# A gather moved into the attention, the last split halved over two engines, and a wait for output moved into the next block

## What is computed

```python
xn = _layernorm(x)
qkv = xn @ Wqkv + bqkv                       # 16 heads of 16
scores = where(abs(i - j) <= 64, q @ k.T / 4, lowest)
attn = softmax(scores) @ v
attention = attn @ Wout + bout
logits = xn @ router_w + router_b            # 8 experts
gating = softmax(logits, all but the top 2 masked out)
h_e = relu(xn @ w1[e] + b1[e])               # 256 -> 1024, for each expert e
moe = sum over e of gating[:, e] * (h_e @ w2[e] + b2[e])
out = x + attention + moe
```

## Time and profile before

| | us |
|---|---|
| median of 3 runs | 963.66 (963.28 to 963.79) |
| the profiled execution, its time | 962.66 |
| its span, first to last instruction | 960.5 |
| PE busy in the span | 901.5 (94%) |
| VectorE busy | 821.9 (86%) |
| ScalarE busy | 739.9 (77%) |
| POOL busy | 494.6 (51%) |
| mean granted TensorE clock | 0.984 |

### The profile page before, as it was taken

How to read it: one execution, slowest core, us unless ns; L and a number is a source line. 1 busy time by engine, 2 the same in 40 slices (tenths; PEclk the granted TensorE clock), 3 DMA queues, 4 the chain that set the end, 5 groups by cost and what they waited for, 6 DMA issues and landing times. The chain is left out here.

```text
span 960.5 us, 27552 instructions
## 1 busy us (share of the span) xinstructions
PE 901.5 (94%) x7684; PEld 874.9 (91%) x7684; DVE 821.9 (86%) x2171; ACT 739.9 (77%) x1983; POOL 494.6 (51%) x699
## 2 busy tenths in 40 slices
PE   4899799899999999999947999999999999999996
PEld 4788789889999999999947999999999999999996
DVE  5876699998888888888846999999999999999995
ACT  4445799889999999999935777777777777677773
POOL 5220013236565555555443666666666666666663
PEclk9999799999999999999987999999999999999999
DMA  4879433344444445444314222222212223222220
GB/s 147 324 276 311 146 78 94 108 124 136 135 134 141 142 136 150 138 133 135 101 46 165 38 39 43 40 41 41 33 29 43 47 46 48 43 44 35 34 24 1
DMA packets 69867, 95.33 MB, mean 99 GB/s; under 512 B 15549, under 2 KB 48960, under 8 KB 69696
## 3 DMA queue, kind: packets, MB, share of 16 engines
q1 hardware_dynamic: 52800, 77.97, 26.4%
q0 software_dynamic: 17024, 16.88, 11.1%
HBM read 62.91 MB, written 35.53 MB: 102 GB/s over the span
## 5 line engine op out<-in xcount | busy, mean ns | idle before, releaser
L1007 ACT ACTIVATE weights_qkv<-weights_qkv,low 128x256 f32<-128x256 f32 (+1 forms) x512 | 240.3, 480 | 1.4 <-DVE low L818 1.4
L1419 ACT ACTIVATE hid<-ps_experts,b_s 128x256 f32<-128x256 f32 x312 | 130.9, 473 | 115.4 <-PE ps_experts L1486 92.2
L1305 POOL DMA_INDIRECT out<-y,target x78 | 149.2, 1912 | 110.5 <-DVE y L1385 94.2
L829 DVE TENSOR_TENSOR pt<-ps_attend,pt 128x512 fp32r<-128x512 f32 (+1 forms) x256 | 158.5, 620 | 39.2 <-ACT pt L1020 26.1
L1097 PE MATMUL ps_attend<-pt,v_m 128*80 128x256 f32 (+7 forms) x1536 | 187.0, 271 | 2.3 <-DVE inv_t L842 1.0
L1502 PE MATMUL ps_experts<-w_hi,h_hi 128*128 128x256 f32 x624 | 175.5, 281 | 1.1 <-DVE h_lo L1352 1.1
L1486 PE MATMUL ps_experts<-xgt_hi,w_hi 128*128 128x256 f32 x624 | 173.3, 278 | 1.7 <-DVE xgt_lo L1343 1.7
L1097 PEld LDWEIGHTS ps_attend<-pt,v_m 128*80 128x80 f32 (+3 forms) x1536 | 170.7, 161 | 4.2 <-issue 4.2
L1486 PE MATMUL ps_experts<-xgt_hi,w_lo 128*128 128x256 f32 x624 | 173.2, 278 | 0.0
L1486 PE MATMUL ps_experts<-xgt_lo,w_hi 128*128 128x256 f32 x624 | 173.0, 277 | 0.0
L1502 PE MATMUL ps_experts<-w_lo,h_hi 128*128 128x256 f32 x624 | 172.4, 276 | 0.0
(11 more groups left out here) (165 smaller groups left out, 2007.9 us busy)
## 6 DMA issues: line engine op xcount, KB each, us to landing
weights_qkv<-in_w SPq DMA_DIRECT2D x15, 1024.0 KB, 6.7
qk_hi<-weights_qkv SPq DMA_DIRECT2D x16, 512.0 KB, 4.7
qk_lo<-weights_qkv SPq DMA_DIRECT2D x16, 512.0 KB, 5.7
q_st<-qk_hi SPq DMA_DIRECT2D x128, 64.0 KB
k_st<-qk_hi SPq DMA_DIRECT2D x128, 64.0 KB
weights_qkv<-in_x SPq DMA_DIRECT2D x8, 512.0 KB, 4.7
xn_rows<-weights_qkv SPq DMA_DIRECT2D x8, 512.0 KB, 5.3
k_st<-qk_lo SPq DMA_DIRECT2D x64, 64.0 KB
```

The source lines that it names most:

```text
L829: v.tensor_tensor(lo[:, f:l], ps[:, bank_t[h], 0:l - f], hi[:, f:l].bitcast(F32), ALU.subtract).then_inc(s_plo, 1)
L1007: ins = act.activation(wt[:, ring, at_tile(i)], wt[:, ring, at_tile(i)], ACT.Exp, bias=low[:, ring, i:i + 1], scale=-1.0, accum_out=total[ ...
L1305: pool.indirect_dma_start(out_tokens, bass.IndirectOffsetOnAxis(ap=target[:, h:h + 1], axis=0), y[:, h], None, bounds_check=T - 1, oob_is_ ...
L1419: ins = act.activation(hid[:, n % 2, j], ps[:, bank_h[n], j * ROWS:(j + 1) * ROWS], ACT.Relu, bias=b1[:, ds(e * FC + 2 * n + j, 1)])
```

## The change

1. The last chunk of the attention: VectorE normalises it in two halves of 256 tokens, ACT makes `a_hi` half by half, VectorE makes `a_lo` half by half, and PE's last products wait for the half that they read. POOL has no part in it any more.
2. The rows of step 0 are gathered by POOL at the end of its queue in the attention, into a buffer `first_rows` that outlives the block and is set to zero in norm_project. `xg(0)` is that buffer in the experts; rings 1 and 2 are a smaller tile, which POOL sets to zero itself at the start of the experts.
3. SP doesn't wait in the attention for the last stores. Their semaphores outlive the block, and SP waits for them before it loads b2, POOL before its first step.
4. `hid`, `gated_b2` and `y` are allocated ahead of `b2`.

```diff
@@ norm_project, POOL
                 pool.memset(g.late, 0.0)
+                pool.memset(g.first_rows[:].bitcast(F32), 0.0)
@@ attend, SP
                 start(sp, by["sp"])
+                start(sp, s_out)
...
                 sp.wait_ge(s_rows, 16 + START)
-                for h in range(2):
-                    sp.wait_ge(s_out[h], 16 * B + START)
                 sp.wait_ge(s_wload, 32 * (E - 1) + 16 + START)
@@ attend, POOL
-                split_output(B - 1, 1, False)
+                pool.wait_ge(s_rows, 16 + START)
+                pool.tensor_copy(g.first_index[:], g.rows[:, 0:2, 0].bitcast(U32)).then_inc(s_first, 1)
+                pool.wait_ge(s_first, 1 + START)
+                for h in range(2):
+                    pool.indirect_dma_start(
+                        g.first_rows[:, h].bitcast(F32), None, g.xn_dram,
+                        bass.IndirectOffsetOnAxis(ap=g.first_index[:, h:h + 1], axis=0),
+                        bounds_check=T - 1, oob_is_err=False).then_inc(g.s_g[h], 16)
@@ attend, VectorE
-                normalise(2 * B - 1)
+                v.wait_ge(s_pv, HC * 2 * B + START)
+                v.wait_ge(s_invs, 2 * B + START)
+                for h in range(2):
+                    v.tensor_tensor(inv_t[:, half_of(h)], ps[:, bank_o, half_of(h)], inv_t[:, half_of(h)], ALU.mult
+                                    ).then_inc(s_enda, 1)
+                for h in range(2):
+                    v.wait_ge(s_endhi, h + 1 + START)
+                    v.tensor_tensor(a_lo[:, 1, half_of(h)], inv_t[:, half_of(h)],
+                                    a_hi[:, 1, half_of(h)].bitcast(F32), ALU.subtract).then_inc(s_endlo, 1)
@@ attend, ACT
                 inverse_out(2 * B - 1, False)
+                act.wait_ge(s_proj, 2 * (B - 1) + START)
+                for h in range(2):
+                    act.wait_ge(s_enda, h + 1 + START)
+                    act.activation(a_hi[:, 1, half_of(h)], inv_t[:, half_of(h)], ACT.Copy).then_inc(s_endhi, 1)
@@ attend, PE, project
-                        if k % 6 == 0 or k == here[0]:
+                        if bank != bank_m and k == 6:
+                            pe.wait_ge(s_endlo, h + 1 + START)
+                        elif k % 6 == 0 or k == here[0]:
@@ experts, tiles
+        hid = sb("hid", [P, 2, 2, ROWS])
+        gated_b2 = sb("gated_b2", [P, 2, D])
+        y = sb("y", [P, 2, D])
         b2 = sb("b2_s", [P, E, D])
...
-        xg = sb("xg", [P, RING, 2, D], F32R)
+        more_rows = sb("more_rows", [P, RING - 1, 2, D], F32R)
@@ experts, SP
                 sp.wait_ge(s_tr, 1 + START)
+                for h in range(2):
+                    sp.wait_ge(g.s_out[h], 16 * B + START)
                 sp.dma_start(b2[:], g.b2.partition_broadcast(P)).then_inc(s_b2, 16)
@@ experts, POOL
-                pool.wait_ge(s_xz, RING + START)
-                for n in range(RING):
+                for ring in range(1, RING):
+                    pool.memset(xg(ring)[:].bitcast(F32), 0.0).then_inc(s_xz, 1)
+                pool.wait_ge(s_xz, RING - 1 + START)
+                for h in range(2):
+                    pool.wait_ge(s_g[h], 16)
+                for n in range(1, RING):
                     gather(n, n, n)
                     for h in range(2):
                         pool.wait_ge(s_g[h], 16 * n + 16)
+                for h in range(2):
+                    pool.wait_ge(g.s_out[h], 16 * B + START)
@@ experts, VectorE
-                for ring in range(RING):
-                    v.memset(xg[:, ring].bitcast(F32), 0.0).then_inc(s_xz, 1)
```

More of the change, by code:

```diff
@@ L561, in attend @@
         s_xb = [sem("s_xb0", "sp"), sem("s_xb1", "sp")]
-        s_out = [sem("s_out0", "sp"), sem("s_out1", "sp")]
+        s_out = g.s_out
         s_wload = sem("s_wload", "sp")
@@ L593, in attend @@
         s_rows = sem("s_rows", "sp")
+        s_first = sem("s_first", "pool")
+        s_enda = sem("s_enda", "v")
+        s_endhi = sem("s_endhi", "act")
+        s_endlo = sem("s_endlo", "v")
         s_sent = ctx.enter_context(nc.semaphore("s_sent"))
@@ L601, in attend, with half_of @@
         out_rows = g.out.rearrange("b (t p) d -> b p t d", p=P)
+        def half_of(h):
+            return slice(2 * P * h, 2 * P * (h + 1))
         def at_tile(i):
@@ L1213, in experts @@
         xt_lo = sb("xgt_lo", [P, DC, ROWS], F32R)
-        hid = sb("hid", [P, 2, 2, ROWS])
         h_hi = sb("h_hi", [P, FC, ROWS], F32R)
         h_lo = sb("h_lo", [P, FC, ROWS], F32R)
-        gated_b2 = sb("gated_b2", [P, 2, D])
-        y = sb("y", [P, 2, D])
         s_b1 = sem("s_b1", "sp")
@@ L1225, in experts @@
         s_landed = sem("s_landed", "sp")
-        s_xz = sem("s_xz", "v")
+        s_xz = sem("s_xz", "pool")
         s_ident_r = sem("s_ident_r", "v")
         s_idx = sem("s_idx", "pool")
-        s_g = [dma_sem("s_g0"), dma_sem("s_g1")]
+        s_g = g.s_g
         s_tr = sem("s_tr4", "pe")
@@ L1250, in experts, with xg @@
         out_tokens = g.out.rearrange("b n d -> (b n) d")
+        def xg(ring):
+            return more_rows[:, ring - 1] if ring else g.first_rows
         def final(s, ahead=1):
@@ L1283, in gather @@
                     pool.tensor_copy(index[:, ring], g.rows[:, ds(2 * row_step, 2), 0].bitcast(U32)).then_inc(s_idx, 1)
-                    pool.wait_ge(s_idx, s + 1 + START)
+                    pool.wait_ge(s_idx, s + START)
                     pool.sem_inc(g.tick, 1)
@@ L1287, in gather @@
                         pool.indirect_dma_start(
-                            xg[:, ring, h].bitcast(F32), None, g.xn_dram,
+                            xg(ring)[:, h].bitcast(F32), None, g.xn_dram,
                             bass.IndirectOffsetOnAxis(ap=index[:, ring, h:h + 1], axis=0),
                             bounds_check=T - 1, oob_is_err=False).then_inc(s_g[h], 16)
-                pool.wait_ge(s_xz, RING + START)
-                for n in range(RING):
+                for ring in range(1, RING):
[4 more added lines that the diff above has]
+                for n in range(1, RING):
                     gather(n, n, n)
@@ L1471, in transpose_rows @@
                             ins = pe.transpose(ps[:, bank_t, (c * 2 + h) * P:(c * 2 + h + 1) * P].bitcast(F32R),
-                                               xg[:, ring, h, c * P:(c + 1) * P], ident_r[:])
+                                               xg(ring)[:, h, c * P:(c + 1) * P], ident_r[:])
                     ins.then_inc(s_tr, 1)
@@ L1553, in build @@
         g.rows = sb("rows", [P, HT, 2])
+        g.first_rows = sb("first_rows", [P, 2, D], F32R)
+        g.first_index = sb("first_index", [P, 2], U32)
+        g.s_g = [ctx.enter_context(nc.semaphore(f"s_g{h}")) for h in range(2)]
+        g.s_out = [ctx.enter_context(nc.semaphore(f"s_out{h}")) for h in range(2)]
         g.step_expert = sb("step_expert", [P, STEPS], I32)
```

## The result

The changed kernel takes 956.93 us (median of 4 runs, 955.02 to 957.31), the kernel before, on the same chip, 963.47 (4 runs, 962.12 to 963.79). The ratio is 0.9935, 95% interval [0.9921, 0.9948]. I forecast 953.3 and a range of 950.9 to 956.2, so the direction is right and the size is not: 6.5 us of gain where I summed 10.4. The profiled execution took 957.17 us with a span of 955.1, against 962.66 and 960.5: 5.4 us of span.

A forecast was written before the change was run, and what follows sets the result against it. It took the experts' steps as bound by TensorE and sought the gain in the 27.3 us around the change of stage: 1.6 + 2.1 + 7.1 - 0.4 = 10.4 us, so 953.3 us, range 950.9 to 956.2.

The forecast's parts named there:

- Part 1: Attention's tail: normalising and splitting in halves without POOL brings TensorE's next product sooner; gain 1.6 us, ends 0.5 to 2.0.
- rival B: Attention's tail: VectorE's two-input subtraction waits out a POOL gather issue on the shared port; 1.1 lost, 954.4; chance 0.12.
- Part 2: Attention's end: SP no longer waits for the last output to land, so the experts start sooner; gain 2.1 us.
- Rival C: Block's end waits for stores or new gather in flight without being told; 2.1 comes back, 955.4; chance 0.10.
- Part 3: Experts' start: first gather hidden in the attention; entry (R) to first expert matmul falls from 11.57 to 4.5, gain 7.1.
- rival E: Experts: step 1's gather comes late beside b2 and weight loads; at 4 us late 955.4; chance 0.05.
- rival F: Experts' steps: VectorE becomes the bound because tiles lie at other addresses; slower, 968.9; chance 0.02.
- The clock: Experts' start: TensorE's clock still falls, low 4.5 us instead of 3.7; loss 0.4, ends gain 1.85 to loss 3.2.
- my signs of being wrong: Transposes waiting for a gather, first stage over 8 us, subtraction over 0.3 us late, or waiting for step 1's gather.

The follow-up runs named there:

- run 7: The split in halves alone, added to the kernel before: 961.35 us, ratio 0.9990.
- run 5: The changed kernel with SyncE's landing wait for the last stores put back in the attention: 955.82 us, ratio 0.9932.
- run 4: The changed kernel with the last batch's two stores issued some 20 us early, sending a weight tile instead: 954.68 us, ratio 0.9920.
- before again: The kernel before, unchanged, profiled once more: 963.17 us (12 runs), ratio 1.0005.
- run 8: The changed kernel with the split in halves undone, so that GpSimd splits first and gathers then: 959.82 us, ratio 0.9973.
- run 10: The changed kernel with GpSimd waiting for its own gather to land before it leaves the attention: 955.71 us, ratio 0.9933.
- run 12: The changed kernel with the table's 66 small scatters left out; experts' rows are skipped: 954.18 us (one run).
- run 13: The kernel before with the table's 66 small scatters left out; experts' rows are skipped: 960.93 us (one run).
- run 11: The kernel of run 7 with GpSimd waiting for its own last addition before it leaves the attention: 962.26 us (one run).
- run 3: The changed kernel with step 0's gather issued earlier, between the heads of the attention's last batch: 954.03 us, ratio 0.9910.
- run 6: The changed kernel with both the gather issued early and SyncE's landing wait put back: 956.71 us, ratio 0.9932.
- run 9: The changed kernel with one small gather more, issued and awaited at the end of the normalisation and projections block: 954.92 us (one run).
- the square of runs: The changed kernel with gather late or early, without or with landing wait; R-n 7.26 (neither), 7.32 (wait), 4.99 (early gather), 7.31 (both).

## Why the prediction missed

**Part 1, the halves: right.** 1.7 at TensorE where I wrote 1.6, in the changed kernel and alone (run 7). VectorE had been idle for 0.21 when its subtraction began at 492.16; by the trace's records that is 0.03 after the end of ScalarE's first pass (492.13), while GpSimd's second issue (491.79 to 492.80) was running, so that rival B did not occur. The Trainium skill's rule of the shared port pair ("SBUF — State Buffer", "SBUF: two separate sides") would allow a loss of up to one issue here; this trace shows no hold of VectorE.

**Part 2, the landing wait: the step that failed.** I wrote "SP no longer waits 2.1 us; it leaves the block with the second store issued", and from that a gain of 2.1 at R. SyncE did leave; R did not follow, and the gain was 0 to 0.1 (run 5). A block closes with its last engine. In the kernel before two of them arrived within 0.3 us of each other: GpSimd's drain ended at 498.32, SyncE at 498.64. I read the one whose wait stood in the earlier trace rows and never asked who was second. One rule gives R within about 0.2 in all nine profiles of this table, and in run 4: the later of SyncE's arrival + 0.2 and GpSimd's last work or wait + 5.65. (An asterisk marks which one decides; n and W as above, for the awaited gather the end of that wait; SyncE's arrival, the drain and R are read from the trace's records of the queues.)

```
kernel            n       W        SyncE arrives   R       R-n
before            489.99  493.00   498.64 *        498.82   8.83
before again      488.13  491.13   496.78 *        496.94   8.81
split alone       488.67  486.86   495.65 *        495.81   7.14
changed           491.19  492.80 * 496.03          498.45   7.26
wait back         490.38  491.98   497.54 *        497.70   7.32
gather early      491.06  489.48   495.89 *        496.05   4.99
early + wait      490.81  489.24   497.96 *        498.12   7.31
split undone      489.04  495.47 * 495.55          501.11  12.07
gather awaited    488.88  492.24 * 493.71          498.10   9.22
```

It explains both of the odd results: the wait that costs nothing (run 5), and the part whose removal costs 4.8 instead of 1.7 (run 8). In the changed kernel the halves paid at R because they took the two split passes off GpSimd, not because TensorE ended sooner. That R-n fell by 1.57, just the 1.6 of the sum, is luck: GpSimd's last work moved from n+3.01 to n+1.61, which is 1.4, and the rest is that SyncE had been 0.2 later still. Rival C has the same price (955.4) and the place, the block's end, but the wrong cause: neither the stores (run 4) nor the gather (run 10) in flight hold it; the drain does, and it is long after the scatters issued in that block (runs 12 and 13).

**Part 3, the gather: right.** R+4.54 for R+4.5, and 7.03 for 7.1. The rows landed long before they were read. Step 1's gather was seen landed at 508.43, before the transposes of step 1 at 511.50 (rival E: no). VectorE's slack in a step is unchanged (rival F: no): from the second product stage of step 0 to the moment at which GpSimd sees the first half of the last step's y are 433.35 us before and 433.60 after.

**The clock: right in kind; its size is chance from profile to profile.** The fall stayed. Of my signs of being wrong one came, a first product stage longer than 8 us. In the profiled pair the dense low time is 5.8 us instead of 3.7, a loss of 0.94 where I took 0.4. Over fourteen profiles it was 3.7 to 5.7 in four with the late entry (the kernel before twice, runs 7 and 11) and 3.7 to 6.2 in ten with an early one (the changed kernel twice, runs 3, 5, 6, 8, 9, 10 and the changed kernel with increments or with the tiles back); from the first matmul to the second product stage they took 8.2 and 8.3 on average. A term of 0.1, then, against my 0.4; my ends (a gain of 1.85 to a loss of 3.2) held both.

**What I did not have in the sum.** First, the 1.2 us ahead of n. Compared operation by operation (ScalarE's), the changed kernel's first profile is behind that of the kernel before by 0.76 us at 22 us, 0.32 at 104, 0.86 at 114, 1.10 at 200 and 1.20 at n. Two things are mixed in this. One goes with the single execution. The low stretch at the attention's start has another length in other profiles of one and the same program: 10.2 us with n at 489.99, 6.8 with n at 488.13, both the kernel before; the 0.6 by which these two differ at 22 us is there as well, before any of it. At 6.8 us, n is 488.1 to 489.3 without the gather in the attention (three profiles) and 488.4 to 489.0 with it (five), no different. At 10.2 or more it is 489.99 in the one profile without and 490.4 to 491.2 in those with it. The longer stretch was there in one of four profiles without and in six of the ten with it, and on average n is 1.0 later in the ten. But these are few profiles. The mean granted clock is recorded for more executions: it is 0.984 or less (the value of the profile with 10.2) in 54 of 88 of the kernel before, and 0.988 or less (the value of the changed kernel's profile with 10.2) in 10 of 15 of the changed kernel. As far as this mean tells, the longer stretch is about as common without the change as with it, and most of the 1.0 is the draw of the profiles.

The other thing is small and steady: between 150 and 170 us every kernel that has the halves or the new gather falls 0.24 to 0.28 behind the kernel before (17 profiles), while the second profile of that kernel and run 13 stay within 0.02 of it; why stays open. Second, the kernel's end, 0.8, and small differences within the steps: from the second product stage to the end 443.0 on average in the four, 443.6 in the ten.

By these averages the change gives 1.6 up to R, 7.1 from R to the first matmul, less 0.1 for the clock, 1.0 ahead of n and 0.6 behind: 7.0, beside the measured 6.5 (interval 5.0 to 7.6). With the steady 0.3 ahead of n instead of the drawn 1.0 it is 7.7, and with the clock's 0.9 of the first pair 6.9. So of the 3.9 that the sum was too high, 2.1 are part 2, shown by the square of runs; about 1 are the kernel's end and the steady 0.3, measured but unexplained; what is left, under 1 us, is within the interval and can't be assigned from these profiles.

## What to carry to other kernels

Where a block closes with a common arrival, list when each engine is done with its last work and its drain before you price the removal of one's wait; what a removal is worth is its distance to the second. GpSimd's work that is needed early in the next block belongs well ahead of this block's end, not behind its last work: moving the two gather issues up by 7 and 10 us gained 2.3 at the entry, and the kernel went from 956.6 to 954.0. Where dense matmuls follow a pause of a few us, matmuls of no use within the pause can be worth as much as a shorter pause: 2.0 us of the first product stage and 2.5 of the span here, beside the 2.3 at the entry.

## What the hardware showed that I had not expected

GpSimd's closing drain ended 5.3 to 5.5 us after its last work in all profiles where it had issued the 66 scatters in the block (5.3 with these alone, 5.5 with the two gathers as well); behind a wait (runs 10 and 11) it took as long from its own start. It was 1.26 with two gathers alone, 0.15 with one awaited gather in another block, and 0.07 with none. At the end of the experts, with some 150 awaited transfers, it took 2.1 to 2.2, so that the number alone does not give the length; what in them does is open. The Trainium skill ("VectorE: DVE Perf Modes", "The DRAIN you can't avoid") tells of boilerplate drains, of the preamble and postamble, with a constant 12 ns or so on all five engines. The drains here close a block of the program: SyncE's took 0.01 us, near that figure, but GpSimd's up to 5.5 us behind its last work, so that the figure does not carry over to them.

The low stretch of TensorE's clock near 100 us was 6.8 us long in one profile of the kernel before and 10.2 in the other (10.2 and 13.7 in two of the changed kernel), and 1.4 of the 1.9 us by which what follows came later with the longer one arose there.
